# Early layer-norm statistics, two multiplies moved to GpSimd, and four output buffers in a fused macaron layer

## Chip, cores and metric

The kernel runs on the 8 cores of one Trainium2 chip. Each core takes one batch element of 2048 tokens by 2048 features and computes the whole layer for it; the cores exchange nothing. The metric is the device time, in microseconds, of the slowest core.

## What is computed

```python
x = x + 0.5 * ffn(layernorm(x))        # top-2 of 8 experts, one 2048x2048 matrix each
x = x + attn(layernorm(x))
x = x + 0.5 * ffn(layernorm(x))

# attn(x), rms = division by the root mean square of a row
q, k, v = split(rms(x) @ w_qkv.T);  q = rms(q);  k = rms(k);  w = exp(k)
y = sigmoid(q) * (cumsum(w * v) / (cumsum(w) + 1e-6))      # sums over the tokens
u, g = split(y @ w_swiglu.T)                               # 8192 wide each
return x + u * silu(g) @ w_out.T
```

## The kernel before

It is written engine by engine: each block of code appends instructions to the queue of one engine, and counting semaphores order the engines. An engine executes its queue in the order in which it was written. `vedge` increments a semaphore with a VectorE instruction and makes VectorE wait for it, so that the next instruction starts when this one has ended.

**FFN (`emit_ffn`, twice), in two halves of 1024 tokens.** ScalarE's queue loads the half of x into `xr` by two transfers of 4 MB (L463), each behind the store of the half before. `emit_ln_batch` then normalises four token tiles of 128, and then the other four: 16 `bn_stats` (L249), 4 `bn_aggr` (L254), Ln and Exp on ScalarE (L261, L262), and for each tile an affine step (L299), 16 transposes (L328) and two copies into `lnTh` (L355). `emit_gating_batch` computes the router: a matmul (L373), forty small VectorE instructions in groups of five for each of eight tiles (L388 to L396), three on ScalarE, sixteen more on VectorE (L415, L418), and transposes of the weights. After the bias the main loop runs 32 blocks (8 experts by 4 column blocks) of 128 matmuls (L534); each block's eight results are accumulated by VectorE into `xr` (L549). GpSimd's queue loads the weights by double buffers (`w_stream`, L176).

**A1 (`emit_a1`).** Two groups of eight tiles: one load of 8 MB (L583), the same layer norm over eight tiles, and the normalised rows added to `xspill` in DRAM by accumulating transfers.

**QKV (`emit_qkv_attn`).** 48 chunks of 64 matmuls (L821). The first 32 give q and k, which go to DRAM. Each of the last 16 (here: V chunks) gives 128 features of v: ScalarE copies the first half of the tokens to `at2` (L870) and half of the rest to `vstrip[0]` (L876), VectorE the last quarter to `vstrip[1]` (L884), SP's queue stores both strips. After each V chunk comes `a3_chain(0, fc)`, the attention chain of the first token half for these features: SP loads q and k (L633, L637), VectorE multiplies them by `rkb` and `rqb` (L662, L664; two column halves each, four multiplies in all), and then ScalarE and VectorE alternate until the product goes to `yT` (L735). GpSimd's queue holds in this section nothing but the weight load of each chunk, which waits for the matmuls of the chunk two before.

**P5 (`emit_p5`).** Two token halves by four groups. In each group an up phase of 16 steps `mi` (a u and a g block of 64 matmuls in all, L1021; silu on ScalarE, L1038; the product to `h_sg` by VectorE, L1046, L1048), and a down phase of 4 column blocks `oq` by 8 token tiles `tc` (L1083), 512 matmuls. The result of a tile is copied from one of two PSUM banks to one of two buffers `tmpout` (L1099) and added to `xspill` by an accumulating transfer (L1109), issued by GpSimd's queue behind the weight load of the next column block (`wob`). In the first up phase, step `mi` begins with `a3_chain(1, mi)`, the chain of the second token half, with v also loaded from DRAM (L644).

Of the kernel before, what the change touches and what calls it, by code (L numbers as in the profile page):

```python
# [41 lines left out]
def build_program(stages=("ffn1", "attn", "proj", "ffn2")):  # L42
# [29 lines left out]
    def nxt(name, shape, dtype):  # L72
# [49 lines left out]
              for i in range(2)]  # L122
# [37 lines left out]
    adp_sems = [S_("adp0"), S_("adp1")]  # L160
# [71 lines left out]
    def emit_ln_batch(srcs, dst_lnT, col_of, rms_fold, accum_rows=None,  # L232
                      sb=0, prev_tr=None, pre_wait=None):
        n = len(srcs)
        L = lnsc
        mean_str = L[:, 2 * sb:2 * (sb + n):2]
        var_str = L[:, 2 * sb + 1:2 * (sb + n):2]
        rsd = L[:, 16 + sb:16 + sb + n]
        scl = L[:, 24 + sb:24 + sb + n]
        bia = L[:, 32 + sb:32 + sb + n]  # L240
        tmp = L[:, 40 + sb:40 + sb + n]

        @blk.vector
        def _(v):
# [11 lines left out]
            vedge(v, ins)  # L256

# [102 lines left out]
    def emit_gating_batch(gbase, lnT_t):  # L360
# [20 lines left out]
        def _(v):  # L381
# [4 lines left out]
            for ci in range(NTH):  # L386
                gl = glog[:, ci * 8:(ci + 1) * 8]
                vedge(v, v.reduce_max(G[:, ci:ci + 1], gl, axis=AX.X))  # L388
                vedge(v, v.tensor_scalar(mk1[:, ci * 8:(ci + 1) * 8], gl,
                                         G[:, ci:ci + 1], None, op0=ALU.is_ge))  # L390
                vedge(v, v.scalar_tensor_tensor(mk2[:, ci * 8:(ci + 1) * 8],
                                                mk1[:, ci * 8:(ci + 1) * 8], -1e30, gl,
                                                op0=ALU.mult, op1=ALU.add))
                vedge(v, v.reduce_max(G[:, 8 + ci:9 + ci],
                                      mk2[:, ci * 8:(ci + 1) * 8], axis=AX.X))
                vedge(v, v.tensor_scalar(mk2[:, ci * 8:(ci + 1) * 8],  # L396
                                         mk2[:, ci * 8:(ci + 1) * 8],
                                         G[:, 8 + ci:9 + ci], None, op0=ALU.is_ge))
# [10 lines left out]
        def _(v):  # L409
            v.wait_ge(s_se.h, s_se.n)  # L410
            vedge(v, v.tensor_scalar_mul(G[:, 24:32], G[:, 24:32], 0.5))
            vedge(v, v.tensor_scalar(G[:, 8:16], G[:, 24:32], -1.0, 0.5,
                                     op0=ALU.mult, op1=ALU.add))
            for ci in range(NTH):
                vedge(v, v.tensor_scalar_mul(mk1[:, ci * 8:(ci + 1) * 8],  # L415
# [31 lines left out]
    def emit_ffn(ffn_idx, xr, src_dram, do_output):  # L447
        for half in range(2):
# [107 lines left out]
            def _(sy):  # L556
                sy.wait_ge(s_ev.h, s_ev.n)
                tgt = y_out if do_output else xspill
                for q in range(2):
# [7 lines left out]
                    spill_all.append((s_slq[q], s_slq[q].n))  # L567

    a1x = at("a1x", [128, NTH * DM], F32, R1)

    def emit_a1():
        ve_group_done = [0]
        for grp in range(2):
# [612 lines left out]
```

## Time and profile before

| | us |
|---|---|
| time, median of 2 runs | 8546.3 (8541.5 to 8551.1) |
| the profiled execution, time | 8567.3 |
| its span (slowest core, core 3) | 8565.7 |
| spans of the eight cores | 8488.9 to 8565.7 |
| TensorE busy | 7282.7 (85%) |
| VectorE busy | 2080.8 (24%) |
| ScalarE busy | 811.1 (9%) |
| GpSimd busy | 764.7 (9%) |

In the trace of core 3, the four main loops of the FFN end at 1070, 2112, 7512 and 8543 us. A1 fills the time to 2364, q and k that to 2815, the V chunks with the first chains run from 2849 to 3170, the last two of these chains and a broadcast to 3226, the first up phase of P5 with the second chains to 3635, and the rest of P5 to 6497. Line numbers such as L1083 are those of the kernel before.

### The profile page before, as it was taken

The numbers are of one execution on the slowest core, as the hardware profiler recorded it, in microseconds if no ns is written. First come the engines' busy times: TensorE is split into PE (matmuls) and PEld (weight loads), VectorE is DVE, ScalarE is ACT, GpSimd is POOL, SyncE is SP. The second block draws the span as 40 slices with busy tenths as digits, with TensorE's granted clock in tenths as the row PEclk, the third lists the DMA queues.
The fourth block names the chain that finished last, engine by engine and source line by source line (L and its number), as shares of the span: only waits on it lengthen the run. The fifth ranks groups of instructions, "written<-read, shape, count | busy, mean of one in ns | idle before, by whom it ended". The sixth has DMA issues, their size and how long they took to land.

```text
span 8565.7 us, 79324 instructions; the slowest of 8 cores (8488.9 to 8565.7 us)
## 1 busy us (share of the span) xinstructions
PE 7282.7 (85%) x33216; PEld 3249.9 (38%) x33216; DVE 2080.8 (24%) x3111; ACT 811.1 (9%) x991; POOL 764.7 (9%) x742
## 2 busy tenths in 40 slices
PE   5999949998199767589889898989894999949998
PEld 2444424443144322233333343434332444424444
DVE  4122242221433455410111101010114222242221
ACT  0000000000022454401001010101010000000000
POOL 0000000000000000021111111111110000000000
PEclk9899969999599878799999999999996999969999
DMA  4455535555766447778787878787785455535444
GB/s 78 61 76 74 77 98 79 78 74 98 154 109 113 82 96 108 103 89 91 78 95 76 98 72 99 74 97 83 87 91 91 69 79 79 74 103 79 74 74 99
DMA packets 1042540, 751.93 MB, mean 88 GB/s; under 512 B 640638, under 2 KB 968446, under 8 KB 1025802
## 3 DMA queue, kind: packets, MB, share of 16 engines
q0 software_dynamic: 998960, 578.93, 55.5%
q1 hardware_dynamic: 39004, 134.37, 5.4%
q10 hardware_dynamic: 4224, 33.55, 1.1%
q8 instruction: 268, 4.39, 0.2%
q14 instruction: 84, 0.69, 0.0%
HBM read 1082.38 MB, written 159.40 MB: 145 GB/s over the span
## 4 chain that ended last, share of the span: by engine, by line
PE 67%; DMA 19%; DVE 7%; issue 3%; ACT 2%; SPq 1%; POOL 0%; DVEq 0%; ACTq 0%; POOLq 0%
PE pb L534 42%; PE pb L1021 12%; PE pb L1083 6%; DMA xspill<-tmpout 6%; PE pb L821 5%; DMA wst<-wuT_blk 4%; DMA at<-qkvd 3%; DMA wst<-wgT_blk 2%; DVE stats_all L249 1%; DVE xr L508 1%; DMA xspill<-a1f 1%; DMA a1x<-xspill 1%; DVE at L715 1%; DVE tmpout L1099 1%; DMA xr<-x 1%
## 5 line engine op out<-in xcount | busy, mean ns | idle before, releaser
L534 PE MATMUL pb<-wblk,lnTh 128*128 128x512 bf16 x16384 | 3596.5, 383 | 11.7 <-DVE xr L508 11.7
L534 PEld LDWEIGHTS pb<-wblk,lnTh 128*128 128x128 bf16 x16384 | 1616.9, 99 | 1992.9 <-issue 198.4
L1021 PE MATMUL pb<-yT,wst 128*128 128x512 bf16 x8192 | 1842.4, 385 | 210.6 <-DMA wst<-wuT_blk 67.8
L549 DVE SCALAR_TENSOR_TENSOR xr<-pb,wm,xr 128x512 f32<-128x512 f32 x1024 | 768.6, 751 | 2831.9 <-PE pb L534 2831.9
L1021 PEld LDWEIGHTS pb<-yT,wst 128*128 128x128 bf16 x8192 | 797.7, 99 | 1256.4 <-issue 364.8
L1083 PE MATMUL pb<-wob,h_sg 128*128 128x512 bf16 x4096 | 951.9, 397 | 263.1 <-DVE tmpout L1099 183.6
L821 PE MATMUL pb<-lnT,wst 128*128 128x512 bf16 x3072 | 697.6, 391 | 84.9 <-ACT vstrip L876 68.0
L1083 PEld LDWEIGHTS pb<-wob,h_sg 128*128 128x128 bf16 x4096 | 412.6, 101 | 802.4 <-issue 364.7
L328 PE MATMUL pb<-ident_bf,ln2tm 128*128 128x128 bf16 x768 | 89.5, 309 | 506.0 <-DVE ln2tm L299 272.4
L176 POOL DMA_DIRECT2D wblk<-expT_blk x128 | 146.4, 1145 | 3903.3 <-PE pb L534 3898.7
L821 PEld LDWEIGHTS pb<-lnT,wst 128*128 128x128 bf16 x3072 | 307.1, 100 | 476.2 <-issue 135.8
L1046 DVE TENSOR_TENSOR h_sg<-pb,silu_t 128x512 bf16<-128x512 f32 x128 | 88.5, 691 | 1579.4 <-ACT silu_t L1039 1579.4
L1099 DVE COPY tmpout<-pb 128x512 f32<-128x512 f32 x256 | 176.9, 691 | 972.9 <-DMA xspill<-tmpout 600.4
L1038 ACT ACT_TABLE_LOAD x128 | 164.2, 1283 | 2458.4 <-PE pb L1021 2458.1
L261 ACT ACT_TABLE_LOAD x10 | 12.8, 1283 | 3417.2 <-DVE lnsc L254 3417.2
L1109 POOL DMA_DIRECT2D xspill<-tmpout x256 | 217.6, 852 | 1106.4 <-DVE tmpout L1099 1098.8
L328 PEld LDWEIGHTS pb<-ident_bf,ln2tm 128*128 128x128 bf16 x768 | 78.1, 143 | 518.1 <-issue 518.1
L176 POOL DMA_DIRECT2D wst<-wuT_blk x128 | 147.6, 1153 | 918.5 <-PE pb L1021 897.2
L176 POOL DMA_DIRECT2D wst<-wgT_blk x128 | 147.4, 1152 | 794.6 <-PE pb L1021 774.6
L836 DVE COPY qkvsb<-pb 128x512 f32<-128x512 f32 x128 | 85.6, 689 | 184.2 <-PE pb L821 177.0
L176 POOL DMA_DIRECT2D wst<-wqkvT_p x48 | 54.9, 1143 | 725.7 <-PE pb L821 723.0
L662 DVE TENSOR_TENSOR at<-at,rkb 128x512 f32<-128x512 f32 x64 | 44.3, 692 | 299.7 <-DMA at<-qkvd 299.0
(102 smaller groups left out, 1804.6 us busy)
## 6 DMA issues: line engine op xcount, KB each, us to landing
wblk<-expT_blk POOLq DMA_DIRECT2D x128, 2048.0 KB, 17.1
wst<-wuT_blk POOLq DMA_DIRECT2D x128, 512.0 KB, 6.5
wst<-wgT_blk POOLq DMA_DIRECT2D x128, 512.0 KB, 6.6
wob<-woutT POOLq DMA_DIRECT2D x32, 2048.0 KB, 19.9
xspill<-tmpout POOLq DMA_DIRECT2D x256, 256.0 KB, 5.6
at<-qkvd SPq DMA_DIRECT2D x160, 256.0 KB, 6.5
qkvd<-qkvsb SPq DMA_DIRECT2D x32, 1024.0 KB, 5.8
wst<-wqkvT_p POOLq DMA_DIRECT2D x48, 512.0 KB, 9.6
```

What stands on the lines that cost most here:

```text
L176: ws["ld"][i % 2].inc(g.dma_start(out=buf[:].rearrange("p (b i) -> p b i", b=nblk), in_=src_ap), 16)
L249: ins = v.bn_stats(stats_all[:, (sb + ci) * 24 + i * 6: (sb + ci) * 24 + (i + 1) * 6], srcs[ci][:, i * 512:(i + 1) * 512])
L328: ins = t.transpose(pbf(bank)[:, i * 128:(i + 1) * 128], ln2_tm[ci % 2][:, dt * 128:(dt + 1) * 128], ident_bf[:])
L534: ins = t.matmul(pb[tc][:], lnTh[:, dt * HALF + tc * 128: dt * HALF + tc * 128 + 128], wblk[bi % 2][:, dt * 512:(dt + 1) * 512], start=(dt ...
L549: ins = v.scalar_tensor_tensor(dst, pb[tc][:], wm[:, tc * 8 + ie: tc * 8 + ie + 1], dst, op0=ALU.mult, op1=ALU.add)
L821: ins = t.matmul(pb[banks[ni]][:], wst[(wsets["C"]["i"] - 1) % 2][:, dt * 128:(dt + 1) * 128], lnT[:, dt * S + ni * 512:(dt) * S + (ni + 1 ...
L1021: ins = t.matmul(pb[banks[ni]][:], wst[(wsets["C"]["i"] - 1) % 2][:, dt * 128:(dt + 1) * 128], yT[:, dt * S + half * HALF + ni * 512: dt * ...
L1038: e.activation(silu_t[:, 0:512], pb[bg[0]][:], AF.Silu)
L1046: v.tensor_tensor(h_sg[:, col:col + 512], pb[bu[0]][:], silu_t[:, 0:512], op=ALU.mult)
L1083: ins = t.matmul(pb[tc % 2][:], h_sg[:, dffc * HALF + tc * 128: dffc * HALF + tc * 128 + 128], wob[(wsets["D"]["i"] - 1) % 2][:, dffc * 51 ...
L1099: ins = v.tensor_copy(tmpout[tc % 2][:], pb[tc % 2][:])
L1109: ins = g.dma_start(out=xspill[rows:rows + 128, oq * 512:(oq + 1) * 512], in_=tmpout[tc % 2][:], accum_op=ALU.add)
```

## The change

It has six parts.

- **Statistics.** `mk_early_stats` makes eight steps. Each has SP load a token tile of 1 MB into a staging buffer (`xstg`, two of them, the loads held back until the transposes of the running half are over), and VectorE compute its `bn_stats` and `bn_aggr`. The steps are put behind every fourth block of the main loop: in each first half for the second half, and in the second half of the first FFN for the first group of A1. Where they have run, `emit_ln_batch` leaves the statistics out; the second halves now wait for both loads before the first affine. In a half without early statistics, the statistics of all eight tiles now come ahead of the first affine.
- **Router.** The forty and the sixteen small instructions are regrouped by kind, with one `vedge` for a kind instead of one for each instruction (the last `is_ge` of the first set has none).
- **Chain multiplies.** The four multiplies by `rkb` and `rqb` move from VectorE to GpSimd's queue.
- **`vstrip[0]`** is copied by VectorE instead of ScalarE.
- **Down phase.** Four `tmpout` buffers instead of two, a count of transfers for each; PSUM banks 6 and 7 instead of 0 and 1.
- **Waits at the ends of the down phase.** It starts when the last silu has ended, and its first tile waits for each piece of `h_sg` singly; the wait for the last `tmpout` copy moves from step 0 of the next up phase to step 1.

```diff
+    def mk_early_stats(src_dram, src_rows, guard_pe, extra_waits=()):
+        marks = {}
+        steps = []
+        for tc in range(8):
+            def step(tc=tc):
+                @blk.sync
+                def _(sy):
+                    sy.wait_ge(s_pe.h, guard_pe)
+                    for s_, n_ in extra_waits:
+                        sy.wait_ge(s_.h, n_)
+                    if tc >= 2:
+                        sy.wait_ge(s_ve.h, marks[tc - 2])
+                    ins = sy.dma_start(
+                        out=xstg[tc % 2][:],
+                        in_=src_dram[src_rows + tc * 128: src_rows + (tc + 1) * 128, :])
+                    s_st2[tc % 2].inc(ins, 16)
+                ld = s_st2[tc % 2].n
+                @blk.vector
+                def _(v):
+                    v.wait_ge(s_st2[tc % 2].h, ld)
+                    for i in range(4):
+                        ins = v.bn_stats(stats_all[:, tc * 24 + i * 6:
+                                                   tc * 24 + (i + 1) * 6],
+                                         xstg[tc % 2][:, i * 512:(i + 1) * 512])
+                    vedge(v, ins)
+                    ins = v.bn_aggr(lnsc[:, 2 * tc:2 * tc + 2],
+                                    stats_all[:, tc * 24:tc * 24 + 24])
+                    vedge(v, ins)
+                    marks[tc] = s_ve.n
...
             for ci in range(NTH):
-                gl = glog[:, ci * 8:(ci + 1) * 8]
-                vedge(v, v.reduce_max(G[:, ci:ci + 1], gl, axis=AX.X))
...
+                ins = v.reduce_max(G[:, ci:ci + 1], glog[:, ci * 8:(ci + 1) * 8],
+                                   axis=AX.X)
+            vedge(v, ins)
...
+            early = early_done[0] if half == 1 else False
+            if not early:
+                emit_ln_stats([xr[:, tc * DM:(tc + 1) * DM] for tc in range(4)],
+                              sb=0, pre_wait=(s_xl2[0], lq[0]))
+                emit_ln_stats([xr[:, tc * DM:(tc + 1) * DM] for tc in range(4, NTH)],
+                              sb=4, pre_wait=(s_xl2[1], lq[1]))
+            else:
+                @blk.vector
+                def _(v):
+                    for q in range(2):
+                        v.wait_ge(s_xl2[q].h, lq[q])
...
+                    if nb >= 2 and nb % 4 == 2 and hook_steps:
+                        hook_steps.pop(0)()
                     nb += 1
...
-        @blk.vector
-        def _(v):
+        @blk.gpsimd
+        def _(g):
+            g.wait_ge(s_ev.h, rqb_ready[0])
             for s in range(2):
-                v.wait_ge(s_qld2[s].h, qld[s])
-                m_d1[s] = mv(v.tensor_tensor(at1[:, cs[s]], at1[:, cs[s]],
+                g.wait_ge(s_qld2[s].h, qld[s])
+                m_d1[s] = mg(g.tensor_tensor(at1[:, cs[s]], at1[:, cs[s]],
                                              rkb[:, cs[s]], op=ALU.mult))
-                m_d3[s] = mv(v.tensor_tensor(at3[:, cs[s]], at3[:, cs[s]],
+                m_d3[s] = mg(g.tensor_tensor(at3[:, cs[s]], at3[:, cs[s]],
                                              rqb[:, cs[s]], op=ALU.mult))
...
                 @blk.vector
                 def _(v):
+                    v.wait_ge(s_pe.h, pe_b + 3)
+                    v.wait_ge(qw_now[0][0].h, qw_now[0][1])
+                    ins = v.tensor_copy(vstrip[0][:], pb[banks[2]][:])
+                    s_ev.inc(ins)
...
-                                if mi == 0:
+                                if mi == 1:
                                     t.wait_ge(s_opv.h, opv_sg_guard)
...
-                        t.wait_ge(s_swh.h, swh_base + 16)
+                        if oq == 0:
+                            t.wait_ge(s_se.h, sil_last)
...
                             for dffc in range(16):
+                                if oq == 0 and tc == 0:
+                                    t.wait_ge(s_swh.h, swh_base + dffc + 1)
                                 ins = t.matmul(
-                                    pb[tc % 2][:],
+                                    pb[6 + tc % 2][:],
...
                         for tc in range(NTH):
+                            j = tc % 4
                             v.wait_ge(s_pe.h, pe_base + tc + 1)
-                            v.wait_ge(s_adp[tc % 2].h,
-                                      (ad_base[tc % 2] + tc // 2) * 16)
-                            ins = v.tensor_copy(tmpout[tc % 2][:], pb[tc % 2][:])
+                            if j in tm_need:
+                                p_, cnt = tm_need[j]
+                                v.wait_ge(s_adp[p_].h, cnt * 16)
+                            ins = v.tensor_copy(tmpout[j][:], pb[6 + tc % 2][:])
                             s_opv.inc(ins)
+                            planned[j] += 1
+                            tm_need[j] = (j, planned[j])
```

## Rows read from the trace of the kernel before

**Rows 1.** Stretches: length, busy time by engine, granted clock, DMA share, GB/s.
```profile
2849.00:3170.00 321.00, 252.47 (x1024) 106.11 (x1024) 173.38 (x261) 177.78 (x236) 17.11 (x15) 0.87 0.50 94
3226.00:3640.00 414.00, 259.33 (x1038) 108.12 (x1039) 211.84 (x320) 200.39 (x256) 36.53 (x32) 0.82 0.74 106
```

**Rows 2.** The same view, the eight down phases: their sum.
```profile
sum 1162.50, PE 966.45 PEld 419.08 DVE 176.38 ACT 0.00 POOL 245.51; mean PE 120.81 PEld 52.38 DVE 22.05 ACT 0.00 POOL 30.69
```

**Rows 3.** Chain of work, one FFN main loop: start us, us, what.
```profile
1225.90 886.02 PE pb L534 x4096
```

**Rows 4.** Timeline: second halves of the first and of the second FFN.
```profile
1121.86 9.59 DVE L249 BATCH_NORM_STATS2 stats_all<-xr 128x6 f32<-128x512 f32 x16 [51.62 <-DMA xr<-x]
...
1134.87 1.34 DVE L299 TENSOR_SCALAR ln2tm<-xr,lnsc 128x2048 bf16<-128x2048 f32 x1 [0.18 <-DVE lnsc L284]
...
1148.15 9.59 DVE L249 BATCH_NORM_STATS2 stats_all<-xr 128x6 f32<-128x512 f32 x16 [0.17 <-DVE lnTh L355]
...
7553.40 9.59 DVE L249 BATCH_NORM_STATS2 stats_all<-xr 128x6 f32<-128x512 f32 x16 [40.66 <-DMA xr<-xspill]
```

**Rows 5.** Second load L463 of these halves: issue ns and time, landing us.
```profile
L463 ACTq DMA_DIRECT2D xr<-x x1: 374/374/374, 1114.2 to 1114.2; - x1
DMA to landing us min/median/max: 25.1/25.1/25.1
...
L463 ACTq DMA_DIRECT2D xr<-xspill x1: 366/366/366, 7548.7 to 7548.7; - x1
DMA to landing us min/median/max: 17.4/17.4/17.4
```

**Rows 6.** Landing of the two loads L463, first half of the first FFN.
```profile
DMA to landing us min/median/max: 19.2/27.8/36.4
```

**Rows 7.** Timeline: statistics of A1's first group.
```profile
2165.72 19.09 DVE L249 BATCH_NORM_STATS2 stats_all<-a1x 128x6 f32<-128x512 f32 x32 [52.95 <-DMA a1x<-xspill]
```

**Rows 8.** Timeline: first of the forty router instructions, and the one behind them.
```profile
83.27 0.16 DVE L388 TENSOR_REDUCE gsc<-stats_all 128x1 f32<-128x8 f32 x1
...
95.43 0.17 DVE L399 TENSOR_TENSOR gsc<-gsc 128x8 f32<-128x8 f32 x1
```

**Rows 9.** Instruction groups by form: count, busy us, mean ns, idle before.
```profile
L249 DVE BATCH_NORM_STATS2 stats_all<-xr 128x6 f32<-128x512 f32 x128 | 76.7, 678 | 145.9 <-DMA xr<-x 76.0 <-DMA xr<-xspill 69.2 <-DVE lnTh L355 0.7
...
L662 DVE TENSOR_TENSOR at<-at,rkb 128x512 f32<-128x512 f32 x64 | 44.3, 692 | 299.7 <-DMA at<-qkvd 299.0 <-DVE rkb L779 0.2
...
L691 DVE TENSOR_TENSOR_SCAN at<-at,stats_all,zeros 128x512 f32<-128x512 f32 x64 | 81.8, 1277 | 0.0
...
L858 DVE TENSOR_TENSOR acck<-acck,sq_t 128x2048 f32<-128x2048 f32 x16 | 36.7, 2292 | 55.3 <-ACT sq_t L853 55.3
```

**Rows 10.** Timeline: one V chunk with its chain (one of sixteen).
```profile
3001.09 0.68 DVE L884 COPY vstrip<-pb 128x512 f32<-128x512 f32 x1
...
3002.27 16.75 PE L821 MATMUL pb<-lnT,wst 128*128 128x512 bf16 x64 [5.92 <-ACT vstrip L876]
...
3009.46 0.69 DVE L662 TENSOR_TENSOR at<-at,rkb 128x512 f32<-128x512 f32 x1 [7.68 <-DMA at<-qkvd]
...
3019.57 1.14 POOL L176 DMA_DIRECT2D wst<-wqkvT_p  x1 [21.53 <-PE pb L821]
```

**Rows 11.** Weight loads L176 between 2849 and 3240 us: landing.
```profile
DMA to landing us min/median/max: 6.4/7.0/13.6
```

**Rows 12.** Timeline: column block 1 of the second down phase.
```profile
4052.12 0.86 POOL L1109 DMA_DIRECT2D xspill<-tmpout  x1 [1.71 <-DVE tmpout L1099]
...
4069.50 0.69 DVE L1099 COPY tmpout<-pb 128x512 f32<-128x512 f32 x1 [12.60 <-DMA xspill<-tmpout]
4070.33 19.92 PE L1083 MATMUL pb<-wob,h_sg 128*128 128x512 bf16 x78 [9.54 <-DVE tmpout L1099]
```

**Rows 13.** Waits, 3640 to 6500 us: total us, times, longest.
```profile
PE pb L1083 <- DVE h_sg L1048: 21.1, 5, 4.2
...
PE pb L1021 <- DVE tmpout L1099: 7.9, 6, 1.9
```

More of the change, by code:

```diff
@@ L230, in build_program, with emit_ln_stats @@
     a1f32 = [at(f"a1f{i}", [128, DM], F32, R3 + 8192 + i * 8192) for i in range(2)]
[L232 to L233 removed]
+    xstg = [at("xstg0", [128, DM], F32, R3), at("xstg1", [128, DM], F32, R3 + 8192)]
+    s_st2 = [S_("st0"), S_("st1")]
+    def mk_early_stats(src_dram, src_rows, guard_pe, extra_waits=()):
[27 more added lines that the diff above has]
+                    marks[tc] = s_ve.n
+            steps.append(step)
+        return steps
+    def emit_ln_stats(srcs, sb, pre_wait=None):
         n = len(srcs)
         L = lnsc
[L236 to L241, printed above, removed]
         @blk.vector
@@ L256, in _, with emit_ln_batch @@
             vedge(v, ins)
+    def emit_ln_batch(srcs, dst_lnT, col_of, rms_fold, accum_rows=None,
+                      sb=0, prev_tr=None, pre_wait=None, skip_stats=False):
+        n = len(srcs)
+        L = lnsc
+        mean_str = L[:, 2 * sb:2 * (sb + n):2]
+        var_str = L[:, 2 * sb + 1:2 * (sb + n):2]
+        rsd = L[:, 16 + sb:16 + sb + n]
+        scl = L[:, 24 + sb:24 + sb + n]
+        bia = L[:, 32 + sb:32 + sb + n]
+        tmp = L[:, 40 + sb:40 + sb + n]
+        if not skip_stats:
+            emit_ln_stats(srcs, sb, pre_wait=pre_wait)
         @blk.scalar
@@ L596, in emit_a1 @@
                                 rms_fold=True, accum_rows=rows,
-                                prev_tr=last_tr[0])
+                                prev_tr=last_tr[0],
+                                skip_stats=(grp == 0 and a1_early[0]))
             last_tr[0] = trg[-2:]
@@ L873, in _ @@
                         ev_at2[ni] = s_ev2.n
-                    e.wait_ge(s_pe.h, pe_b + 3)
-                    e.wait_ge(qw_now[0][0].h, qw_now[0][1])
-                    ins = e.activation(vstrip[0][:], pb[banks[2]][:], AF.Copy)
-                    s_ev2.inc(ins)
                 ev2_t = s_ev2.n
@@ L978, in emit_p5 @@
         pending = []
-        planned = [s_adp[0].n // 16, s_adp[1].n // 16]
+        planned = [s_.n // 16 for s_ in s_adp]
+        tm_need = {}
         nD_blocks = [0]
@@ L1123, in build_program, with a1_factory @@
     if "ffn1" in stages:
-        emit_ffn(0, xr1, x_in, do_output=(stages == ("ffn1",)))
+        if "attn" in stages:
+            def a1_factory(guard_pe):
+                a1_early[0] = True
+                return mk_early_stats(xspill, 0, guard_pe,
+                                      extra_waits=[p for p in spill_q[0]] +
+                                                  [p for p in spill_q[1]])
+            emit_ffn(0, xr1, x_in, do_output=False, post_hook_factory=a1_factory)
+        else:
+            emit_ffn(0, xr1, x_in, do_output=(stages == ("ffn1",)))
     if "attn" in stages:
```

85 lines of the change are left out of this document (54 added, 31 removed).

## The prediction

> **What bounds the kernel now.** I read the busy time of the stretches first, then the chain of waits, then the timelines around the edits. TensorE sets the pace nearly everywhere. An FFN main loop is a solid block of 4096 matmuls in 886.0 us, 0.2163 us each [rows 3]; nothing in the change shortens it, nor the q and k chunks. What can move lies between: the layer norm and router ahead of each FFN loop, where TensorE idles; the V chunks, where 1024 matmuls take 321 us with TensorE 252 us busy, and the first up phase, 414 us with 259 busy, granted clock 0.87 and 0.82 in the means [rows 1]; and the eight down phases, 1162.5 us together [rows 2], against 8 x 512 x 0.2163 = 886 at the FFN's pace: 276 too many.
>
> **Statistics.** In a second half now, from the landing of the first load: 1134.87 - 1121.86 = 13.0 to the first affine, 13.3 for four tiles, 13.0 again for the second statistics, 13.3 for the other tiles: 52.6 [rows 4]. After: from the landing of the second load 0.6 (two small instructions), twice 13.3 and 0.4 between, since the second Ln and Exp run beside the first tiles: 27.6. The gain is 25.0 less the spread of the landings. In the first FFN the second load lands at 1114.2 + 25.1 = 1139.3, 17.4 behind the first: gain 7.6. In the second, 7548.7 + 17.4 = 7566.1, 12.7 behind: gain 12.3 [rows 4, 5]. At the kernel's start the order is worse: the second load lands 17.2 + 0.5 (its issue) behind the first [rows 6], the first statistics need 10.4 of that, so VectorE waits 7.3 before it may go on, and gets 2.6 back from the hidden Ln and Exp: loss 4.7. The first half of the second FFN I take at 0. A1's first group loses its 19.1 of statistics [rows 7], the aggregates (1.1) and one Ln and Exp (2.1): gain 22.3. Sum: -37. The steps themselves (2.7 us of VectorE behind every fourth block) are free: a bank is used again 8 x 3.46 us later, and VectorE works 0.75 in each 3.46. Without that cover they would cost 24 x 3.1 = 74. SP has nothing else queued there. Their 24 MB lie under loops whose weights are far ahead.
>
> **Router.** Forty instructions take 95.43 - 83.27 = 12.2, 0.30 each [rows 8]. Unfenced instructions overlap: sixteen `bn_stats` of 0.678 follow each other every 0.599 [rows 4, 9], 0.08 less than they last. At a mean length of 0.19 the forty would need 0.11 each plus five fences of 0.2, 5.2 in all; without overlap 8. The sixteen later ones scale the same. Saving 7.0 + 2.9, four times: -38 (between -24 and -42).
>
> **V chunks: the part that costs.** What moves is four multiplies, but into the queue that loads the weights. Now that queue waits only for matmuls: the load issued at 3019.57, when the chunk begun at 3002.27 is over, is for the chunk after the next, and the next one is already there [rows 10]. After the change the order in GpSimd's queue is: weights k, multiplies k, weights k+1. The multiplies of chain k need q and k, whose loads stand in SP's queue behind the stores of chunk k's strips, and these behind chunk k's matmuls. So the weights of k+1 are asked for only after chunk k has been computed; the double buffer is gone, and everything is in series:
> - 64 matmuls with a cold start 16.4 (16.75 shown; 13.8 at full clock);
> - last copy to the first multiply: 3009.46 - 3001.09 = 8.4 [rows 10];
> - four multiplies. The trace shows none on GpSimd. Bounds: VectorE's 0.692 for the same shape; 2.292 for four times the elements [rows 9]. I take 1.28, as the scan, VectorE's slowest op of this shape: 5.1;
> - the weights, 7.0 to land (6.4 to 13.6) [rows 11], and 0.3 of semaphores.
>
> Period 37.2, against (321 - 16.7) / 15 = 20.3 now; fifteen periods: 15 x 16.9 = +253. At 0.692 it is +218, at 2.292 +314. Weights that land in 13.6 would add 99, but nothing else loads at that moment. The `vstrip` copy moved to VectorE ends 0.35 later than ScalarE's and is inside this. Behind the last matmul two chains run now; after it only one: -21.
>
> The Trainium skill (GPSIMD Engine Reference, "Performance versus the Vector engine") calls GpSimd the wrong place for elementwise work and measures a two-input add of 2048 elements at 4497 ns against VectorE's 2293. The 2292 ns of this trace agree with its VectorE figure; by its ratio of 1.96 one multiply would be 1.36, an estimate, and the V chunks would cost 5 more.
>
> **First up phase.** Here the multiplies need no matmuls of their own step, only the chain before. From one chain's end D: q, k and v landed 8.9 (6.3 for four transfers in the V chunks, half as many again), multiplies done 12.2, weights landed 20, two blocks of matmuls done 36, silu 38.5, and the next but one chain, whose ScalarE work stands behind this silu, ends 12 later, at D + 50.5: 25.2 per step, where it is 414 / 16 = 25.9 now [rows 1]. I take 0, with +30 at 2.292 and +50 if the loads collide.
>
> **Down phases.** Now a stall comes whenever a `wob` load is issued ahead of the transfers: the one issued at 4052.12 lets VectorE go on at 4069.50, 17.4 later, and TensorE has idled 9.5 [rows 12]; two such in each phase, a smaller one at the third load, and a cold clock behind each (78 matmuls in 19.92, 3.0 over pace). With four buffers VectorE needs that transfer four tiles later (13.8) and TensorE can run two tiles more in the banks; from one copy on, the transfer is issued 1.2 later, its buffer is free 17.4 after that, the next copy takes 0.8, and TensorE has had five tiles (5 x 3.46 = 17.3, less 0.2 of lead) to compute: the stall is 19.4 - 17.1 = 2.3, with the clock 3.5. A phase becomes 110.7 + 2 x 3.5 + some 5 for loads and starts = 122.5 instead of 145.3: -182. Bounds: -100, if the same transfers, crowded into less time, land late; -250, if no stall is left. The earlier start saves the two products of `h_sg`, 1.3 of each wait of 4.2, 8 times: -10; the moved wait, 7.9: -8 [rows 13]. Together -200.
>
> **Sum.** -37 - 38 + 253 - 21 + 0 - 200 = -43. The profiled execution took 8567.3, so it would take 8524; it stands 21 above the median, and against the median of 8546.3 the time is 8503.
>
> **Rivals.**
> - *The multiplies are much slower on GpSimd.* Each further us of one costs 4 x 15 = 60 in the V chunks and about 40 in the up phase. From 3.4 us on the kernel is slower by over 2%; at 4 us: 8503 + 272 = 8775. For it: no such row. Against it: a shape of four times the elements takes 2.3 on VectorE.
> - *The weights are not held up*, as if the load could pass the multiplies: the V chunks keep their pace but for some 1.5 us a chain. 8503 - 253 + 24 = 8274. For it: only that four multiplies are little work. Against it: the code's order.
> - *The down phases are bound by the transfers, not by the buffers.* 32 transfers and the weights stay the same; then a phase gains some 5 us: 8503 + 140 = 8643. For it: the transfer that waits for `wob` would be as late. Against it: outside these moments it lands before the second next tile.
> - *No stall is left* in the down phases: 8503 - 75 = 8428.
>
> **Chances.** Forecast 0.62, slow multiplies 0.09, weights not held 0.07, transfers bind 0.13, no stall 0.09. Range: from 8410, no stall, to 8650, transfers bind. The measurement tells about 2%, 171 us, from no change. Below 8375: the second rival and a little of the last, 0.09. Above 8717: the first rival, or the third with a costly GpSimd, 0.12. Within: 0.79.
>
> **What would show it.** V chunks: TensorE waiting for `wst` loads, periods of 37, weight loads issued right behind a multiply on GpSimd. Down phases near 122 with stalls of 2 to 3. Statistics inside the main loops, 27 us from the second landing to the router's matmul. Wrong I would be by the multiply's length, by weights that land faster than 6.4, or by down phases that stay above 135.

## The result

The time is 0.994 of that before, with a 95% interval of 0.992 to 0.996: about 8497 us against 8546.3, a difference of under 2%. It is taken from five executions of the kernel after, 8474 to 8492 us, and six of the kernel before, 8510 to 8551. Most executions of both kernels had a lower granted clock on one die or on both, which adds several per cent to either; every comparison below is between executions without it or, where a kernel had none, between its cores or stretches without it.

The profiled execution took 8487.8 us. Its slowest core is core 1, with a span of 8486.0; the eight spans lie between 8450.0 and 8486.0, and their median is 8466, where it was 8514. From the page of the profile after (busy us, share and instructions by engine; then groups: count, busy, mean ns of one, idle before and its releaser):

```profile
span 8486.0 us, 79400 instructions; the slowest of 8 cores (8450.0 to 8486.0 us)
PE 7202.9 (85%) x33216; PEld 3235.3 (38%) x33216; DVE 2020.6 (24%) x2999; ACT 805.0 (9%) x975; POOL 934.7 (11%) x870
L1173 PE MATMUL pb<-wob,h_sg 128*128 128x512 bf16 x4096 | 922.6, 389 | 100.3 <-DVE tmpout L1191 52.3
L906 PE MATMUL pb<-lnT,wst 128*128 128x512 bf16 x3072 | 703.9, 394 | 310.4 <-DMA wst<-wqkvT_p 307.7
L746 POOL TENSOR_TENSOR at<-at,rkb 128x512 f32<-128x512 f32 x64 | 80.4, 1257 | 795.9 <-DMA at<-qkvd 776.2
L775 DVE TENSOR_TENSOR_SCAN at<-at,stats_all,zeros 128x512 f32<-128x512 f32 x64 | 101.9, 1591 | 0.0
```

L906 is now the QKV matmul, L1173 the one of the down phases, L746 and L748 are the moved multiplies. TensorE waits 307.7 us for QKV weights, where core 3 of the kernel before waited 14.2:

```profile
L821 PE MATMUL pb<-lnT,wst 128*128 128x512 bf16 x3072 | 697.6, 391 | 84.9 <-ACT vstrip L876 68.0 <-DMA wst<-wqkvT_p 14.2 <-DVE rkb L779 2.7
```

One multiply on GpSimd takes 1.257 us (L746). The last section tells why those of L748 take 1.398 in the mean.

The two traces cut at the same matmuls, as medians over the eight cores, beside the terms of the prediction:

| stretch | before | after | measured | predicted |
|---|---|---|---|---|
| start to the first main loop | 130.0 | 125.3 | -4.7 | +4.7 - 9.5 = -4.8 |
| between main loops 1 and 2 | 155.1 | 138.1 | -17.0 | -7.6 - 9.5 = -17.1 |
| A1 | 253.2 | 232.5 | -20.7 | -22.3 |
| q and k | 484.5 | 484.2 | -0.3 | 0 |
| V chunks | 320.2 | 547.3 | +227.1 | +253 |
| last V matmul to the first up matmul | 56.9 | 44.9 | -12.0 | -21 |
| first up phase and its gap | 398.2 | 393.5 | -4.8 | 0 |
| eight down phases | 1137.0 | 976.1 | -160.9 | -182 |
| seven later up phases | 1652.2 | 1655.4 | +3.2 | 0 |
| seven gaps, up to down | 31.8 | 31.5 | -0.3 | -10 (eight of them) |
| seven gaps, down to up | 19.8 | 10.9 | -8.9 | -8 |
| entry of the second FFN | 134.8 | 124.5 | -10.3 | -9.5 |
| between main loops 3 and 4 | 149.2 | 130.2 | -19.0 | -12.3 - 9.5 = -21.8 |

The measured column adds up to -28.6, the predicted one to -43. The median span fell by 48; the 20 between come from two main loops of before, whose mean over the cores was 899.3 and 893.2 us in that execution, where 886 is usual. Four cores were longer there; core 2 ran its first loop at a granted clock of 0.82 and 0.87 up to 500 us, and at 1.00 behind. That is no effect of the change. Without it the traced execution of before stands at about 8498 in the median of its cores, and ten others beside the experiments at 8512 to 8537 (the kernel after: five at 8460 to 8466). So the -28.6 is what two traced executions differ by; the times differ by 49.

**The V chunks.** The timeline of core 1, one chunk with its chain (start us, us, engine, line; idle before and its releaser):

```profile
2815.70 1.25 POOL L746 TENSOR_TENSOR at<-at,rkb 128x512 f32<-128x512 f32 x1 [30.47 <-DMA at<-qkvd]
2819.12 0.83 DVE L771 TENSOR_TENSOR at<-at,at 128x512 f32<-128x512 f32 x1 [10.04 <-ACT at L755]
2819.37 1.71 POOL L748 TENSOR_TENSOR at<-at,rqb 128x512 f32<-128x512 f32 x1
2819.88 2.28 DVE L775 TENSOR_TENSOR_SCAN at<-at,stats_all,zeros 128x512 f32<-128x512 f32 x1
2821.03 1.19 POOL L176 DMA_DIRECT2D wst<-wqkvT_p  x1
...
2827.91 16.84 PE L906 MATMUL pb<-lnT,wst 128*128 128x512 bf16 x64 [19.70 <-DMA wst<-wqkvT_p]
...
2844.93 0.69 DVE L969 COPY vstrip<-pb 128x512 f32<-128x512 f32 x1 [2.76 <-PE pb L906]
...
2851.61 1.25 POOL L746 TENSOR_TENSOR at<-at,rkb 128x512 f32<-128x512 f32 x1 [29.40 <-DMA at<-qkvd]
```

Everything is in series. Multiplies from 2815.70 to 2821.03, 5.3; weights issued then and used at 2827.91, 6.9; matmuls up to the last copy of `vstrip`, 17.0; store, load of q and k, and the next multiply at 2851.61, 6.7. Together 35.9, where the period was 20.3. In [rows 10] the weight load was put out when a chunk ended and lay one chunk ahead.

**A down phase.** Core 1, column block 1 of the first down phase, and the sum over its eight down phases by stretches (length, then busy us by engine):

```profile
3785.70 1.52 POOL L176 DMA_DIRECT2D wob<-woutT  x1
3787.39 0.69 DVE L1191 COPY tmpout<-pb 128x512 f32<-128x512 f32 x1 [2.76 <-PE pb L1173]
3788.62 0.86 POOL L1203 DMA_DIRECT2D xspill<-tmpout  x1 [1.40 <-DVE tmpout L1191]
...
3807.29 0.69 DVE L1191 COPY tmpout<-pb 128x512 f32<-128x512 f32 x1 [8.84 <-DMA xspill<-tmpout]
3808.13 30.36 PE L1173 MATMUL pb<-wob,h_sg 128*128 128x512 bf16 x128 [3.64 <-DVE tmpout L1191]
```

```profile
sum 974.80, PE 922.46 PEld 408.67 DVE 171.74 ACT 0.00 POOL 246.03; mean PE 115.31 PEld 51.08 DVE 21.47 ACT 0.00 POOL 30.75
```

The accumulating transfer issued right behind a `wob` load (3788.62) lets VectorE go on 18.7 us later, about as in [rows 12]; but three copies into other buffers fit in between instead of one, and TensorE idles 3.64 instead of 9.54.

The 1162.50 of [rows 2] is not to be set beside this sum: its windows reach over the ends of the phases. Cut from the first to the last matmul of each phase, core 3 of the kernel before gives:

```profile
sum 1135.60, PE 951.63 PEld 412.29 DVE 171.33 ACT 0.00 POOL 243.42; mean PE 118.95 PEld 51.54 DVE 21.42 ACT 0.00 POOL 30.43
```

**Layer norm and router.** Second half of the first FFN, core 1, from the landing of the second load to the router's matmul; and of its first half the first and the last of the forty regrouped instructions:

```profile
1081.52 0.17 DVE L326 COPY lnsc<-lnsc 128x4 f32<-128x4 f32 x1 [68.81 <-DMA xr<-x]
...
1109.41 3.55 PE L416 MATMUL pb<-gateT_bf,lnTh 128*128 128x8 bf16 x128 [1.05 <-DVE lnTh L398]
```

```profile
88.36 0.64 DVE L430 TENSOR_REDUCE gsc<-stats_all 128x1 f32<-128x8 f32 x8
...
92.99 0.16 DVE L452 TENSOR_TENSOR gsc<-gsc 128x8 f32<-128x8 f32 x1
```

27.9 us from the landing to the router's matmul, and 4.6 us for the forty, which took 12.2 in [rows 8].

### The profile page after: what moved, and what is told of

Read it like the earlier page. It is cut to its first block, busy times and chain, and to the rows that moved or that the text cites. A ratio compares the mean times of both kernels' runs of the same rounds, so it can differ in the third digit from the quotient of the medians.

```text
span 8486.0 us, 79400 instructions; the slowest of 8 cores (8450.0 to 8486.0 us)
## 1 busy us (share of the span) xinstructions
PE 7202.9 (85%) x33216; PEld 3235.3 (38%) x33216; DVE 2020.6 (24%) x2999; ACT 805.0 (9%) x975; POOL 934.7 (11%) x870
## 4 chain that ended last, share of the span: by engine, by line
PE 71%; DMA 20%; DVE 4%; issue 3%; ACT 1%; POOL 1%; SPq 0%; DVEq 0%; POOLq 0%; ACTq 0%
PE pb L605 42%; PE pb L1107 12%; PE pb L906 8%; PE pb L1173 8%; DMA wst<-wuT_blk 5%; DMA xspill<-tmpout 4%; DMA wst<-wgT_blk 2%; DMA wob<-woutT 2%; DMA at<-qkvd 2%; DMA wst<-wqkvT_p 1%; DMA xspill<-a1f 1%; DVE xr L579 1%; DMA xspill<-xr 1%; DMA a1x<-xspill 1%; DMA xr<-x 1%
## 5 line engine op out<-in xcount | busy, mean ns | idle before, releaser
L605 PE MATMUL pb<-wblk,lnTh 128*128 128x512 bf16 x16384 | 3546.6, 380 | 11.7 <-DVE xr L579 11.7
L1173 PE MATMUL pb<-wob,h_sg 128*128 128x512 bf16 x4096 | 922.6, 389 | 100.3 <-DVE tmpout L1191 52.3
L906 PE MATMUL pb<-lnT,wst 128*128 128x512 bf16 x3072 | 703.9, 394 | 310.4 <-DMA wst<-wqkvT_p 307.7
L1173 PEld LDWEIGHTS pb<-wob,h_sg 128*128 128x128 bf16 x4096 | 407.9, 100 | 615.0 <-issue 157.5
L906 PEld LDWEIGHTS pb<-lnT,wst 128*128 128x128 bf16 x3072 | 308.3, 101 | 706.9 <-issue 370.5
L176 POOL DMA_DIRECT2D wblk<-expT_blk x128 | 146.4, 1145 | 3798.5 <-PE pb L605 3793.7
L176 POOL DMA_DIRECT2D wst<-wuT_blk x128 | 148.6, 1161 | 670.4 <-PE pb L1107 670.4
L176 POOL DMA_DIRECT2D wst<-wgT_blk x128 | 147.7, 1154 | 645.2 <-PE pb L1107 644.1
L746 POOL TENSOR_TENSOR at<-at,rkb 128x512 f32<-128x512 f32 x64 | 80.4, 1257 | 795.9 <-DMA at<-qkvd 776.2
L775 DVE TENSOR_TENSOR_SCAN at<-at,stats_all,zeros 128x512 f32<-128x512 f32 x64 | 101.9, 1591 | 0.0
```

The lines of the kernel that those rows point to most:

```text
L176: ws["ld"][i % 2].inc(g.dma_start(out=buf[:].rearrange("p (b i) -> p b i", b=nblk), in_=src_ap), 16)
L605: ins = t.matmul(pb[tc][:], lnTh[:, dt * HALF + tc * 128: dt * HALF + tc * 128 + 128], wblk[bi % 2][:, dt * 512:(dt + 1) * 512], start=(dt ...
L775: m_d4[s] = mv(v.tensor_tensor_scan(at4[:, cs[s]], at1[:, cs[s]], zeros[:, 0:SUBW], carry_w[:, fc:fc + 1], op0=ALU.add, op1=ALU.add))
L906: ins = t.matmul(pb[banks[ni]][:], wst[(wsets["C"]["i"] - 1) % 2][:, dt * 128:(dt + 1) * 128], lnT[:, dt * S + ni * 512:(dt) * S + (ni + 1 ...
L1173: ins = t.matmul(pb[6 + tc % 2][:], h_sg[:, dffc * HALF + tc * 128: dffc * HALF + tc * 128 + 128], wob[(wsets["D"]["i"] - 1) % 2][:, dffc ...
```

## The experiments

They stand in the order in which they ran. Times of stretches are medians over the cores, cut as in the table above.

### e1: the multiplies back on VectorE

```diff
-        @blk.gpsimd
+        @blk.vector
         def _(g):
-            g.wait_ge(s_ev.h, rqb_ready[0])
...
-                m_d1[s] = mg(g.tensor_tensor(at1[:, cs[s]], at1[:, cs[s]],
+                m_d1[s] = mv(g.tensor_tensor(at1[:, cs[s]], at1[:, cs[s]],
```

> The changed kernel with its four chain multiplies back on VectorE's queue, the rest of the change kept. If the multiplies in GpSimd's queue are what the V chunks pay for, the stretch of the V chunks goes from 547 us back to about 320, the way from its end through the first up phase from 438 to about 455, and the whole is about 210 us faster than the changed kernel: near 8290, 0.970 of the kernel before. If instead the longer V stretch came from the vstrip copy moved to VectorE or from the other edits, which stay here, it remains above 500 us and the kernel near 8490.

The V chunks took 330.2 us instead of 547.3, the stretch behind them 58.7 instead of 44.9. The others are near those of the changed kernel; the largest difference is in the down phases, 992.5 for 976.1. Two executions took 8343.1 and 8356.4 us, with 8555.5 for the kernel before on the same chip. So one of the six parts of the change costs about what the five others gain. The V chunks stay 10 us above the 320.2 of before. The scan, in the groups by form, for the last section:

```profile
L774 DVE TENSOR_TENSOR_SCAN at<-at,stats_all,zeros 128x512 f32<-128x512 f32 x64 | 81.7, 1277 | 0.0
```

### e2: the multiplies stay on GpSimd, the weight load goes ahead of them

```diff
             qkv_chunk(i, jc, None)
+            if fc + 1 < ND:
+                load_chunk(jc + 1)
             a3_chain(0, fc, v_in_at2=True)
```

`load_chunk` is the `w_stream` call of a chunk, put here for the next V chunk.

> The changed kernel with the multiplies still on GpSimd, but in the V chunks the weight load of the next chunk is put into GpSimd's queue ahead of the multiplies instead of behind them. Theory of the queue: the double buffer is back, the V stretch falls from 547 us to 320 plus what the slower multiplies add to each chain, about 1.3 us, so to about 340, and the kernel to about 8300. Theory of the slow engine (the multiplies, or their contention with VectorE, are the cost): the V stretch stays above 450 us and the kernel above 8400.

The V chunks took 345.7 us, with the multiplies as slow as before. The move costs 217 in this kernel (547.3 - 330.2, e1), and 202 of them are gone. The spans of cores 4 to 7 are 8263 to 8296 us, where a time of about 8300 was expected. Core 5:

```profile
2852.30 1.26 POOL L746 TENSOR_TENSOR at<-at,rkb 128x512 f32<-128x512 f32 x1 [16.59 <-DMA at<-qkvd]
...
2855.97 1.72 POOL L748 TENSOR_TENSOR at<-at,rqb 128x512 f32<-128x512 f32 x1
2857.65 1.20 POOL L176 DMA_DIRECT2D wst<-wqkvT_p  x1
...
2864.24 16.85 PE L912 MATMUL pb<-lnT,wst 128*128 128x512 bf16 x64 [6.54 <-DMA wst<-wqkvT_p]
...
2874.52 1.25 POOL L746 TENSOR_TENSOR at<-at,rkb 128x512 f32<-128x512 f32 x1 [15.68 <-DMA at<-qkvd]
2879.86 1.20 POOL L176 DMA_DIRECT2D wst<-wqkvT_p  x1
```

The period is 22.2. The load at 2857.65 still stands behind four multiplies, but behind those of the chain before, which run while a chunk is computed; TensorE waits for it, 6.54, but no longer for the whole row. This settles it: the price was the place of the load in the queue, not the length of a multiply. What is left, 345.7 - 330.2 = 15.5, is the longer multiplies and the wait for this load together.

### e3: only the multiplies are moved, in the kernel before

```diff
-        @blk.vector
+        @blk.gpsimd
         def _(v):
+            v.wait_ge(s_ev.h, rqb_ready[0])
...
-                m_d1[s] = mv(v.tensor_tensor(at1[:, cs[s]], at1[:, cs[s]],
+                m_d1[s] = mg(v.tensor_tensor(at1[:, cs[s]], at1[:, cs[s]],
```

> The kernel before with this one part of the change alone: the four multiplies on GpSimd's queue. Theory of the queue: the V stretch goes from 320 to about 547 us, the rest of the way to the first down phase gets about 17 shorter, and the kernel takes 8546 + 210 = 8756, 1.025 of the kernel before. If the loss in the changed kernel came from the multiplies together with another part (the vstrip copy, the statistics), it is smaller here, under 100 us.

V chunks 552.2, +232; the stretch behind them 45.2, -11.7; the time 8762.5 against 8555.5. The part alone costs 207 us (one execution of each on that chip), and it does not need the others to do so.

### e4: two output buffers, otherwise e1

```diff
-              for i in range(4)]
+              for i in range(2)]
...
-                            j = tc % 4
+                            j = tc % 2
```

> As the kernel with the multiplies back on VectorE, but with two tmpout buffers instead of four; the PSUM banks and the waits at the start of the down phase are those of the change. If the buffers gave the gain of the down phases, their sum goes back from 976 us to about 1137 and the kernel is 161 us slower than with four. If the gain came from the other edits of the down phase, the sum stays below 1020.

The eight down phases took 1144.5 us, against 992.5 in e1 and 1137.0 before: the gain of the down phases is that of the buffers, and banks 6 and 7 with the moved waits give the phases nothing. The gaps from down to up stayed at 10.9, so those 8.9 us belong to the moved wait. Core 5, the sum over its down phases, and its wait for the copies (total us, times, longest):

```profile
sum 1152.30, PE 953.59 PEld 412.78 DVE 172.63 ACT 0.00 POOL 242.03; mean PE 119.20 PEld 51.60 DVE 21.58 ACT 0.00 POOL 30.25
```

```profile
PE pb L1172 <- DVE tmpout L1190: 178.3, 41, 10.7
```

### e5: e1 with the old order of the layer norm

In a first half the statistics of a group of four tiles again come right ahead of its affine steps, and in a second half the first affine waits for the first load only.

```diff
-            if not early:
-                emit_ln_stats([xr[:, tc * DM:(tc + 1) * DM] for tc in range(4)],
-                              sb=0, pre_wait=(s_xl2[0], lq[0]))
-                emit_ln_stats([xr[:, tc * DM:(tc + 1) * DM] for tc in range(4, NTH)],
-                              sb=4, pre_wait=(s_xl2[1], lq[1]))
-            else:
+            if early:
                 @blk.vector
                 def _(v):
-                    for q in range(2):
-                        v.wait_ge(s_xl2[q].h, lq[q])
+                    v.wait_ge(s_xl2[0].h, lq[0])
```

> On top of the kernel with the multiplies on VectorE: the first halves take their statistics in the old order (four tiles, their transposes, four tiles), and the second halves begin with the first load alone and wait for the second before the fifth tile. If the order is what the first half loses 4.7 us by, the first main loop begins 5 us earlier, near 121 us. If waiting for both loads is what the second halves lose, the ways between the main loops shrink by the spread of the landings, 17 us in the first FFN (139 to 122) and about 13 in the second (127 to 114). If the router's transposes or the bias behind them are the limit instead, they stay.

The start fell from 126.0 to 120.8, the two stretches between main loops from 139.1 to 125.7 and from 126.9 to 110.6, the entry of the second FFN from 127.3 to 122.6; the time was 8285.9. So the loss of 4.7 that the prediction gave the new order at the start is there (5.2), and waiting for both loads costs a second half 13 and 16 us.

### e6: e5 with six output buffers

```diff
-              for i in range(4)]
+              for i in range(6)]
...
-                            j = tc % 4
+                            j = (ncopy[0] + tc) % 6
```

> As the kernel with the old order of the layer norm, with six tmpout buffers instead of four. If the stalls behind the wob loads are a matter of buffers, six cover 17.4 us of landing in full and the eight down phases fall from about 980 to near 905 us (886 is the FFN's pace). If the transfers themselves now bind, the sum stays above 960 us.

The down phases took 905.6 us, 113.2 each, the time was 8200.05. Core 5, the same sum, and what TensorE waits for in P5:

```profile
sum 909.20, PE 903.79 PEld 405.14 DVE 173.28 ACT 0.00 POOL 243.37; mean PE 112.97 PEld 50.64 DVE 21.66 ACT 0.00 POOL 30.42
```

```profile
PE pb L1173 <- DMA wob<-woutT: 40.0, 7, 7.2
...
PE pb L1173 <- DVE tmpout L1191: 5.2, 5, 2.7
```

On the cores shown, the waits for a copy are 178.3 us with two buffers, 52.3 with four, 5.2 with six. The transfers themselves bound none of these down phases.

### e7: e5 with the first `wob` load ahead of step 14

```diff
+                    if mi == 14 and not (half == 0 and sg == 0):
+                        load_d(sg, 0)
```

> As the kernel with the old order of the layer norm, with the first wob load of each down phase but the first put into GpSimd's queue ahead of the weights of step 14 of the up phase instead of behind those of step 15. If the down phase now begins when this load has landed, the seven ways from an up to a down phase fall from about 35 us together to about 20 (2.6 to 3 each: silu alone). If they are bound by silu, they stay. The load may delay weights of the last steps; then the seven up phases grow by up to 10 us together.

The gaps from up to down fell to 20.1 as expected, but the seven up phases grew by 67 to 1731.7 (the range of the cores is 1708.7 to 1742.3, against 1647.8 to 1696.2 in e1), where 10 at most was expected; 8351.5 us in all, worse than e5. The gain is real and is paid back elsewhere; where, e11 shows.

### e8: e6 and e7 together, and `vstrip[0]` again on ScalarE

```diff
+                    ins = e.activation(vstrip[0][:], pb[banks[2]][:], AF.Copy)
+                    s_ev2.inc(ins)
...
-                    ins = v.tensor_copy(vstrip[0][:], pb[banks[2]][:])
-                    s_ev.inc(ins)
```

> All that the theories call gains: multiplies on VectorE, vstrip[0] on ScalarE again, the old order of the layer norm, six buffers, the earlier wob load. If the vstrip copy is what the V chunks still lose (330 us against 320 before), they take 320 again. Sum against the kernel before by the stretches: -9.5 at the start, -34 and -35 between the main loops, -17 in A1, 0 in the V chunks, -230 in the down phases, -20 around them, -10 at the second FFN: about -355, so near 8190, 0.958 of the kernel before. If the transfers bind the down phases, about 8270.

Down phases 898.3, up phases 1727.7, gaps 20.1, V chunks 326.8; two executions of 8239.2 and 8247.0, about 0.963 of the 8555 or so of before. That is 50 above the 8190 expected and above e6: the early `wob` load takes its 60 to 70 us in the up phases here too, which the sum left out. The V chunks with the copy on VectorE were 323.5 in e6 and 330.2 in e1, so the copy is not what lifts them over 320.2. That rest of 3 to 10 us stays open.

### e9: e6 once more, for an interval

> The same kernel as e6_six_buffers (changed kernel with the multiplies on VectorE, the layer norm of a first half in the old order, a second half that waits for its first load only, six tmpout buffers), timed in five rounds for an interval. Measured so far: 8200 us in one execution beside 8555 for the kernel before, so a ratio of 0.958. Expected: 0.955 to 0.965, down phases 905 us together, V chunks 320 to 333. It would stand below e8_best (0.963 in the executions seen) by what the early wob load costs there in the up phases.

The ratio to the kernel before is 0.962, with an interval of 0.959 to 0.965 (executions of 8221.1 and 8227.8; before 8537 to 8561 on that chip). Down phases 907.4, V chunks 327.9. This is the fastest version found: the changed kernel without the move to GpSimd, with the old layer-norm order and two buffers more. The 0.963 of e8 lies inside the interval, so the times alone do not tell the two apart; the medians over the cores do, 8174 and 8183 here and 8217 and 8222 in e8.

### e10: four more multiplies in every chain

```diff
                 g.wait_ge(s_qld2[s].h, qld[s])
+                for _r in range(2):
+                    mg(g.tensor_tensor(at4[:, cs[s]], at1[:, cs[s]],
+                                       rkb[:, cs[s]], op=ALU.mult))
+                    g.wait_ge(s_gp.h, s_gp.n)
```

> The changed kernel with four more GpSimd multiplies in each chain (same shape, each waited for singly, results not used): the price of a slower multiply by itself. If the multiplies of a chain stand in series with the matmuls and the weight load, as my theory has it, each of the fifteen periods of the V chunks grows by four times 1.25 to 1.35 us: V chunks 547 to between 622 and 628, and the wait behind the last V chunk grows by 5. For the first up phase my prediction priced a further us of one multiply at about 40, so here 1.25 us more each gives 394 to about 445. The rival, multiplies hidden beside other work, leaves V at 547 and the up phase at 394; a third reading, hidden in the up phase only, gives 625 and 394.

Core 0 took 637.9 us for the V chunks, 545.9 without the extra multiplies, and 462.0 from the first up matmul to the first down matmul, where it had 400.9. A chain of this kernel on core 0:

```profile
2990.25 2.66 POOL L747 TENSOR_TENSOR at<-at,rkb 128x512 f32<-128x512 f32 x2 [29.66 <-DMA at<-qkvd]
2993.05 1.26 POOL L750 TENSOR_TENSOR at<-at,rkb 128x512 f32<-128x512 f32 x1
2994.27 1.26 POOL L752 TENSOR_TENSOR at<-at,rqb 128x512 f32<-128x512 f32 x1
...
2995.49 2.94 POOL L747 TENSOR_TENSOR at<-at,rkb 128x512 f32<-128x512 f32 x2
...
2998.57 1.99 POOL L750 TENSOR_TENSOR at<-at,rkb 128x512 f32<-128x512 f32 x1
...
3000.53 1.26 POOL L752 TENSOR_TENSOR at<-at,rqb 128x512 f32<-128x512 f32 x1
...
3001.74 1.19 POOL L176 DMA_DIRECT2D wst<-wqkvT_p  x1
...
3008.44 16.39 PE L910 MATMUL pb<-lnT,wst 128*128 128x512 bf16 x63 [25.13 <-DMA wst<-wqkvT_p]
```

Eight multiplies take 3001.74 - 2990.25 = 11.5 where four took 5.3, and 6.2 x 15 = 93 is the 92 by which the V chunks grew. So multiplies and matmuls are in series, one for one; nothing hides them. The size was above the expected 75 to 80, because one extra multiply costs 1.54 and not 1.25 to 1.35. Each is waited for singly: two of them take 2.80 up to the next (2993.05 - 2990.25), 1.40 each, where the others follow each other every 1.22. Four are 5.6, and the rest of the 6.2 is VectorE's work beside them, of which the last section tells. The up phase grew by 61 on core 0, where 51 was expected, for 6.2 in each of its sixteen chains: 0.62 of a full series, and 10 for each us, or 39 for each us of one multiply. The prediction priced that at about 40. (Against the median of the eight cores, 393.5, cores 0 to 3 grew by 67 to 70, 44 for each us.)

### e11: the first `wob` load ahead of step 15 only, otherwise e6

```diff
+                    if mi == 15 and not (half == 0 and sg == 0):
+                        load_d(sg, 0)
```

> As e9_six_again, with the first wob load of each down phase issued ahead of the weights of up step 15 (e7_wob_earlier had it ahead of step 14: gaps 20 instead of 36 us, the seven later up phases 67 longer, with four buffers). If a 2 MB load ahead of a step's weights costs that step what the load takes in the queue, wherever it stands, the up phases grow by 67 again and the total is 50 above e9. If the cost comes from transfers of the down phase before or from two steps being late, it is less with one step behind it: up phases +20 to +40, gaps 20 to 34, total within 15 us of e9.

The gaps fell to 20.1 and the down phases to 893.6, but the up phases took 1731.9, 70 more: as much as in e7. The cost is the same at both places. Cores 0 to 3 have a median span of 8210 us, 26 above cores 4 to 7 of e9, where the expectation gave 50 for this theory. The timeline of core 1, end of the second up phase:

```profile
3846.47 1.15 POOL L176 DMA_DIRECT2D wob<-woutT  x1
3847.57 15.76 PE L1125 MATMUL pb<-yT,wst 128*128 128x512 bf16 x64 [2.79 <-DMA wst<-wuT_blk]
3856.87 1.14 POOL L176 DMA_DIRECT2D wst<-wuT_blk  x1 [9.26 <-PE pb L1125]
...
3874.32 16.42 PE L1125 MATMUL pb<-yT,wst 128*128 128x512 bf16 x64 [10.99 <-DMA wst<-wuT_blk]
3893.61 6.69 PE L1182 MATMUL pb<-wob,h_sg 128*128 128x512 bf16 x24 [2.87 <-ACT silu_t L1143]
```

Behind the 2 MB of `wob`, the 0.5 MB of u weights issued at 3856.87 are used at 3874.32, 17.5 later instead of the usual 6.6, and TensorE idles 10.99: seven times that is 77, the 70 that were lost. A step of an up phase has no slack for a weight load that comes this late. One doubt of the prediction is answered on the way: with `wob` there in time, the down phase starts 2.87 behind the last up matmul, where it was 4.2 [rows 13]. The earlier start does give 1.3 us.

## Where the prediction went wrong, and what held

**What failed.** 8503 was predicted and 8497 measured, but that the totals agree so closely is luck: terms that missed cancel. The step that failed is the cost of the V chunks, +253 predicted and +227 measured: its term "last copy to the first multiply" was mis-sized, 8.4 us taken from one chunk where the runs showed 6.7. Opposite to it stands the gain of the down phases, -182 predicted and -161 measured, because the base of 145.3 us for a phase is 142.0. One smaller step failed in its mechanism: the earlier start of the down phases gave nothing instead of 10 us, because the `wob` load is late next.

**What held.** The kernel moved by little, and for the reason given: a loss of over 200 in the V chunks against gains of about the same elsewhere.

**V chunks, +227 for +253.** The chain of the argument (weights behind multiplies, multiplies behind loads, loads behind matmuls) is shown three times: by the waits, by e2, which changes only the order and takes 202 us away, and by e10, which lengthens one link. The rival that weights are not held up fell with the first trace. The length of a multiply, the one price no row gave, was taken as 1.28 and is 1.257; the rival of slow multiplies is out. The term that was mis-sized is last copy to first multiply: 6.7 for 8.4. It was read from [rows 10], where a weight load of another chunk is in flight at that moment; now none can be. The loads do land sooner: in the median of 70 chunks on five cores the first multiply starts 4.7 us after the second of the two loads that it needs is issued, where it was 5.7. That the missing weight load is the reason is not shown: 15 of the 70 chunks of before have one in flight for less than 1 us, and take 8.2 from the copy to the multiply as the others do. The weights took 6.9 for 7.3. Against these stand 0.6 for the matmuls (17.0 to the last copy for 16.4) and 0.2 for the multiplies: 35.9 for 37.2, and 1.3 x 15 = 20 of the 26.

The Trainium skill (GPSIMD Engine Reference, "Performance versus the Vector engine") puts a two-input add on GpSimd at 1.96 times VectorE's time. The multiply here takes 1.257 against 0.692, 1.82 times, so the trace about agrees. That the move costs six times more than the difference (0.565 x 64 = 36 us of multiplies in the V chunks, beside 227) comes from the queue (e2).

**Behind the V chunks, -12 for -21.** One chain instead of two, as said; e3 shows the same 45. The time of the saved chain was put too high. Together with the up phase (-4.8 for 0) the stretch misses by 4.

**First up phase, -4.8 for 0.** The sum came out, but two moves stand behind it that the prediction did not tell apart. From the first to the last up matmul the phase grew (medians 389.6 for 368.3), and the wait before the first down matmul fell from 30.0 to 3.0; the largest before, on core 3, was 47.8. In e3 the two are 393.8 and 4.1, and their sum is again that of before, so both come with the multiplies. The first down matmul, core 3 before and core 1 after:

```profile
3634.68 25.56 PE L1083 MATMUL pb<-wob,h_sg 128*128 128x512 bf16 x107 [47.81 <-DVE h_sg L1048]
...
3753.30 51.19 PE L1173 MATMUL pb<-wob,h_sg 128*128 128x512 bf16 x224 [3.69 <-DMA wob<-woutT]
```

**Down phases, -161 for -182.** The time after was right: 122.0 each (976.1 / 8), predicted 122.5, and the rivals of a transfer bound and of no stall are both out (e4, e6). The term that was mis-sized is the base of 145.3. It comes from [rows 2], whose windows reach over the ends of the phases and take in 15 us of other matmuls (TensorE 966.45 us busy, 951.63 within the phases). Cut at its own matmuls, the same core 3 takes 1135.6 / 8 = 142.0, and the median of the cores is 142.1 (1137.0 / 8). With 142.0 the term would have been 8 x 19.5 = -156. For the same reason the 276 us too many are 250. The single stall was priced at 2.3 and was 3.64 here, 1.42 at the next load; core 1's sixteen waits for a copy are 52.3 us, 3.3 each, so what a phase needs beside them was put too high. The landing was 18.6 and 16.4 for an assumed 17.4.

**Earlier start of the down phase, 0 for -10.** This one had the right size (e11: 1.3 each) and the wrong place. With the products out of the way the next thing that is late is the `wob` load, which was hidden behind them: core 1's waits for it grew from 25.0 us in 5 to 48.0 in 8. The prediction asked "what is late next" for the buffers but not here. And the obvious repair costs more than it gives (e7, e11).

**Statistics and router.** All terms within 3 us: 27.9 from the second landing for 27.6, 4.6 for 5.2 in the forty, 20.7 for 22.3 in A1. Two sums of the router do not add up as written: 0.11 x 40 and five fences of 0.2 are 5.4, and (7.0 + 2.9) x 4 is 39.6, not 38; that is 2 us. The steps inside the main loops are free, as argued: 886 before and after. What the prediction did not ask is whether the second halves had to wait for both loads. It priced that wait (27.6 behind the second landing, not the first) without naming it as a loss; it is 13 and 16 us (e5).

## What to carry to other kernels

Before work is moved to an idle engine, read what its queue is for: GpSimd was 91% idle, but its queue held the weight loads, and four instructions of 1.26 us that wait for late data turned a double buffer into a series. If they must be there, put the load ahead of them; here that is worth 202 of 217 us. Where a stall stems from one late transfer in a steady row, count how many tiles it is late and give so many buffers: two, four and six gave 1144, 992 and 906 us.

## What the runs showed of the hardware

**GpSimd and VectorE hold each other up.** The scan takes 1.277 us in the mean of 64 cases, and 1.280 at most, when the multiplies are on VectorE (e1); with the multiplies on GpSimd it takes up to 2.286, and 101.9 us in sum for 81.7. GpSimd's own fourth multiply takes 1.71 instead of 1.25 in the timeline shown above. The spans fit an exclusive turn: VectorE's product begun at 2819.12 would end by itself at 2819.81; the multiply begun at 2819.37 takes 0.46 too long, up to 2821.08; the scan begun at 2819.88 takes 1.00 too long. In e10 it adds 0.28 to a pair of extra multiplies (2.94 for 2.66) and 0.73 to the next one (1.99 for 1.26), against 0.46 in a chain without extra ones: 5.6 + 0.28 + 0.73 - 0.46 = 6.15 of the 6.2. The Trainium skill (SBUF — State Buffer, "Who interferes with whom") says that a VectorE instruction with two inputs in SBUF contends with a GpSimd instruction that reads SBUF, for a pair of ports that is an exclusive lock; the trace agrees, to within 0.2 us for the scan. The price is small: of the sixteen V chains of core 1, fifteen take 5.37 or 5.38 us for their four multiplies, and the one without a collision 4.92.

**A transfer issued right behind a 2 MB load is late, small or not.** 256 KB behind a `wob` load landed after 18.6 and 16.4 us in the first down phase (16.2 to 20.2 in all sixteen cases of core 1), and in e11 512 KB of weights were used 17.5 after their issue; the medians over all are 6.2 and 6.6. The prediction had read this for the accumulating transfers, not for the weights of the up phase.
